# Attention: a new order of row statistics, k's transposes and exponentials, and block ends whose barrier leaves out GpSimd's drain

## The reference, cut to what matters

```python
h = _L0_tok_ref(x)
h = h + _L0_attn_ref(_layernorm(h, axis=-1), wq, wk, wv, wo)
h = h + _L0_ffn_ref(_layernorm(h, axis=-1), w1, w3, w2)
h = h + _L1_attn_ref(_layernorm(h, axis=-1), Wq, Wk, Wv, Wo)
h = h + _L1_ffn_ref(_layernorm(h, axis=-1), gate_up, down)
# one attention, per batch row of 32 tokens:
q, k, v = x @ wq.T, x @ wk.T, x @ wv.T
q, k = rope(q), rope(k)                  # first attention only
att = softmax(causal(q @ k.T * scale))
out = (att @ v) @ wo.T
```

## Time and profile before

| what | us |
|---|---|
| median of 3 runs (lowest, highest) | 2550.73 (2550.29, 2552.34) |
| profiled execution, its time | 2551.09 |
| profiled execution, span of its instructions | 2549.0 |
| TensorE busy (share) | 2265.7 (89%) |
| VectorE busy | 1679.7 (66%) |
| ScalarE busy | 1491.9 (59%) |
| GpSimd busy | 984.8 (39%) |

### The profile page before, as it was taken

One profiled execution on the slowest core, in us unless ns is written; L12 is line 12 of the kernel. 1 busy time (PEld: TensorE's weight loads), 2 busy tenths in 40 slices (PEclk: granted clock), 3 DMA queues, 4 the chain that ended last, 5 costly groups with the idle time before them and its releaser, 6 DMA issues. The chain is left out here.

```text
span 2549.0 us, 43850 instructions
## 1 busy us (share of the span) xinstructions
PE 2265.7 (89%) x13188; PEld 1134.8 (45%) x13188; DVE 1679.7 (66%) x2922; ACT 1491.9 (59%) x2374; POOL 984.8 (39%) x997
## 2 busy tenths in 40 slices
PE   7999999947999994489999995999996899999997
PEld 2333333314666663234444442666662344444443
DVE  6666666635777775575444682566656888788873
ACT  4666666635777775474222662667654666666663
POOL 2222222216766771142000360444433555455552
PEclk9999999978999997699999997999998999999999
DMA  4555454433321110122111223222211111111101
GB/s 120 132 133 131 129 132 131 115 101 125 116 70 62 62 58 29 51 75 76 50 53 49 89 79 101 68 86 74 83 58 43 34 42 46 38 47 44 42 26 50
DMA packets 144174, 194.53 MB, mean 76 GB/s; under 512 B 32549, under 2 KB 76165, under 8 KB 144058
## 3 DMA queue, kind: packets, MB, share of 16 engines
q1 hardware_dynamic: 117434, 159.58, 20.8%
q10 hardware_dynamic: 26624, 33.56, 4.8%
HBM read 125.17 MB, written 42.21 MB: 66 GB/s over the span
## 5 line engine op out<-in xcount | busy, mean ns | idle before, releaser
L330 DVE TENSOR_REDUCE tm_negmax<-tm_s 128x1 f32<-128x512 f32 x512 | 323.2, 678 | 167.5 <-PE tm_s L374 167.3
L291 ACT ACTIVATE tm_prob<-tm_s 128x1024 f32<-128x1024 f32 x256 | 257.8, 1023 | 140.9 <-PE tm_s L394 136.3
L2001 PE MATMUL f_part<-f_xhi,gu 128*128 128x512 f16 x704 | 269.8, 383 | 14.4 <-ACT f_firstg L1822 4.2
L2001 PE MATMUL f_part<-f_xlo,gu 128*128 128x512 f16 x704 | 268.9, 382 | 0.0
L411 PE MATMUL tm_o<-tm_prob,tm_vt 128*64 128x512 f32 x1024 | 255.4, 620 | 0.0
L2023 PE MATMUL f_pz<-dn,f_ghi 128*128 128x512 f16 x704 | 216.3, 383 | 27.7 <-ACT f_zc L1854 27.7
L1791 POOL TENSOR_TENSOR f_firstg<-f_firstg,f_secondg 128x512 f32<-128x512 f32 x88 | 148.6, 1688 | 198.3 <-DVE f_secondg L1897 198.3
L374 PE MATMUL tm_s<-tm_qk 96*128 96x512 f16 x512 | 199.2, 391 | 14.9 <-DMA tm_qk<-tm_xs 14.3
L248 POOL TENSOR_TENSOR tm_hn<-tm_nd,tm_rows 128x1024 f32<-128x1024 f32 x32 | 75.2, 2351 | 311.3 <-DMA tm_rows<-rden 311.3
L394 PE MATMUL tm_s<-tm_qk 98*128 98x512 f16 x512 | 194.1, 382 | 0.6 <-DMA tm_qk<-tm_mrow 0.6
L971 PE MATMUL a_bankB<-a_wqkv,a_xhi 128*128 128x512 f16 x512 | 159.2, 394 | 2.8 <-DVE a_xlo L821 2.8
(11 more groups left out here) (188 smaller groups left out, 5730.9 us busy)
## 6 DMA issues: line engine op xcount, KB each, us to landing
tm_qk<-tm_xs SPq DMA_DIRECT2D x384, 64.0 KB, 2.1
tm_xqk<-in_qk ACTq DMA_DIRECT2D x32, 512.0 KB, 4.5
a_hin<-h SPq DMA_DIRECT2D x64, 256.0 KB, 2.6
a_hres<-h SPq DMA_DIRECT2D x64, 256.0 KB, 2.7
h<-a_hout SPq DMA_DIRECT2D x64, 256.0 KB, 2.0
f_hin<-h SPq DMA_DIRECT2D x64, 256.0 KB, 2.8
f_hres<-h SPq DMA_DIRECT2D x64, 256.0 KB, 2.8
tm_vt<-in_vt ACTq DMA_DIRECT2D x32, 256.0 KB, 2.9
```

The source lines that it names most:

```text
L291: nc.scalar.activation(prob[b][:, 2 * h:2 * h + 2, :], s2[:, i % 2, :, :], ACT.Exp, scale=SCALE).then_inc(exp_done, 1)
L330: nc.vector.tensor_reduce(negmax[u][:, m:m + 1], s1[:, p % BANKS, :], AX.X, ALU.max, negate=True).then_inc(s1_read, 1)
L2001: last = nc.tensor.matmul(part[q % BANKS][:, :], (gate, up)[which][:, j, m * P:(m + 1) * P], xparts[x][u][:, j, :], start=x == 0, stop=x == 1)
```

## The change

Four edits in `attention`, and one on the ends of all blocks:

1. `row_stats`, `mean_variance` and `variance_eps` move on VectorE from the head of the step to behind `shift`, and serve tile n+5 instead of n+4. The wait for the loaded rows moves with them.
2. On TensorE the transposes of k become a function of their own, `transpose_k`, which stands behind `weigh_values(n - 1)` instead of ahead of it.
3. In the attention with rotation `exps(n)` stands on ScalarE ahead of `copy_q(n + 2, u)` instead of behind it. In the other attention ScalarE's order is as before.
4. `nc.Block()` becomes `nc.Block(no_gpsimd_drain=True)` six times: at the end of a block GpSimd issues no drain of its own; on the other four engines what was one drain with the barrier's semaphores is a drain and a semaphore instruction.

The diff, with one of the six block lines; the other five read the same:

```diff
--- before.py
+++ after.py
@@ -133,7 +133,7 @@
 
         MAXIMA_AT = {11: 0, 3: 1}
         VALUES_AT = {7: 0, 11: 1, 15: 2, 3: 3}
-        block = ctx.enter_context(nc.Block())
+        block = ctx.enter_context(nc.Block(no_gpsimd_drain=True))
 
         def unit(i):
 
@@ -737,9 +737,9 @@
                 n = 2 * k + u
                 copy_qT(n + 1)
                 copy_kT(n + 1)
+                exps(n)
                 if rope:
                     copy_q(n + 2, u)
-                exps(n)
                 y_hi(n - 1)
                 if not rope:
                     copy_q(n + 2, u)
@@ -770,8 +770,9 @@
             nc.vector.tensor_tensor(wo[1][:, :, :], wostage[:, :].rearrange("p (r n) -> p r n", r=R),
                                     wo[0][:, :, :], ALU.subtract).then_inc(w_ready, 1)
 
-            def row_stats(t, u):
-                if inside(t, TILES):
+            def row_stats(t, u, half):
+                if inside(t, TILES):
+                    wait(dve, h_in[u], 16 * (half + 1))
                     nc.vector.bn_stats(stats[u][:, :], hin[u][:, :]).then_inc(s["stats_done"], 1)
 
             def mean_variance(t, u):
@@ -874,17 +875,15 @@
 
             def step(k, u):
                 n = 2 * k + u
-                if inside(n + 4, TILES):
-                    wait(dve, h_in[u], 16 * (k + 3))
-                row_stats(n + 4, u)
-                mean_variance(n + 4, u)
-                variance_eps(n + 4, u)
                 k_lo(n + 1, 1 - u)
                 residual(n - 2, u, k - 1)
                 maxes(n)
                 inverse_sums(n - 1)
                 normalise(n - 1)
                 shift(n)
+                row_stats(n + 5, 1 - u, k + 2 + u)
+                mean_variance(n + 5, 1 - u)
+                variance_eps(n + 5, 1 - u)
                 turn(n + 2, u, 0)
                 y_lo(n - 1)
                 turn(n + 2, u, 1)
@@ -899,7 +898,7 @@
             pe.wait_ge(set_up, 8)
             pe.wait_ge(w_ready, KT)
 
-            def transpose_qk(t):
+            def transpose_q(t):
                 if inside(t, TILES):
                     wait(pe, s["qlo_done"], t + 1)
                     wait(pe, s["qT_copied"], t)
@@ -910,6 +909,9 @@
                                                        qs[:, r, f * G:(f + 1) * G, :, :]
                                                        .rearrange("p g a d -> p (g a d)"), ident16[:, :])
                     last.then_inc(s["qT_ready"], 1)
+
+            def transpose_k(t):
+                if inside(t, TILES):
                     wait(pe, s["klo_done"], t + 1)
                     wait(pe, s["kv_copied"], t + 1)
                     for a in range(2):
@@ -1005,8 +1007,9 @@
             def step(k, u):
                 n = 2 * k + u
                 scores(n)
-                transpose_qk(n + 1)
+                transpose_q(n + 1)
                 weigh_values(n - 1, 1 - u)
+                transpose_k(n + 1)
                 project(n + 2, u, bankB[:, 0:DQ], slice(0, DQ), "q_ready", "out_done", n - 1)
                 transpose_y(n - 1)
                 project(n + 2, u, bankC[:, 0:2 * DKV], slice(DQ, DALL), "kv_ready", "kT_act", n + 2)
```

## The result

| | before | changed |
|---|---|---|
| median, 20 runs each | 2551.64 us (2549.36 to 2554.26) | 2555.09 us (2551.96 to 2560.16) |
| ratio | | 1.0014, 95% interval 1.0008 to 1.0020 |
| profiled execution | 2551.09, span 2549.0 | 2553.93, span 2552.1 |

The forecast was 2550.4 with 0.67 on "no change". The time lies inside the range of 2544 to 2556, but the kernel is slower by more than the runs leave in doubt: 3.5 us instead of -0.3.

A forecast was written before the change was run, and what follows sets the result against it. TensorE bounds the second attention's loop; a chain through VectorE and the exponentials would close the first's. Starts +4.8, steps behind them -1.3 and -1.8, loop -2.0, ends 0: -0.3 us, median 2550.4; range 2544 to 2556 (8 in 10).

The forecast's parts named there:

- no change: Whole kernel: time within 0.2% of before, 5.1 us, about what the runs can tell; chance 0.67.
- The loop: First attention's 22 steps: each takes 12.14 us against 12.23, so 2.0 us gained.
- The ring: First attention's loop: `k_lo`, residual, maxima, reciprocal, products, `shift`, `exps`, `copy_q` set the step, 12.14 us.
- The other parts of the table: Parts outside the first loop: first attention's start and first steps +1.4, second's +0.3 us, the rest 0.
- `k_lo` behind `q_lo`: First attention's loop: `k_lo` on VectorE ends 0.28 us after GpSimd's `q_lo`, at 7.13 into the step.
- the rule that it weighed: Rival, first loop: `k_lo` runs whole behind `q_lo`, step 12.28, loop loses 1.1 us, total 2553.5; chance 0.12.
- The starts: Both attentions' starts: moved statistics delay the first `x_lo` by 2.7 and 2.1 us; 4.8 us lost in all.
- The steps behind the starts: First steps of both attentions: waits at k's and the probabilities' transposes go, 1.3 us gained in the first, 1.8 in the second.
- The block ends: Six block ends: GpSimd's drain is hidden behind the last store; 0 taken, between 3 us gained and 0.3 lost.
- the wait for k simply goes: Rival, first loop: step falls to TensorE's 11.56 or near it, 9 to 15 us less, 2537 to 2543; chance 0.13.
- miss its gap: Rival, first loop: `vhi` holds `k_lo`; every step 13.37, total 2577; chance 0.06, wholly or in some steps.
- The ends: Rival, block ends: they do more than forecast, up to 3 us less, 2547; chance 0.04.

## Why the prediction was wrong

**The loop, the step that failed in size and sign.** The ring, the only thing that could decide it, was named link by link, and each link is in the trace. The step "12.14 against 12.23" was mis-sized by 0.21: 1.06 for the way from the exponentials to q's copy is the row of another pair (`exps` to `y_hi`), where the next instruction overlaps the end of `exps` by 0.1; `copy_q` does not (1.17 to 1.18 in the changed kernel and in three experiments with this order). And "nothing in the edits moves `k_hi` against `copy_q`" overlooked that edit 3 brings `turn(..., 1)` into `cross`, 0.10. Against a margin of 0.09 a step, 0.21 turns the sign: 22 x 0.21 = 4.6 us, more than the 3.7 between forecast and result. The other parts of the table miss theirs by -1.2, +0.7, +5.1, -5.1, -1.4 and +1.0, which nearly cancel; that the total is off by under 0.2% is in part luck.

**`k_lo` behind `q_lo`**: right, 0.28 forecast and 0.29 measured. The forecast took the 0.28 as speaking against the rule that it weighed (the Trainium skill, SBUF — State Buffer, "SBUF: two separate sides": whichever starts first keeps the shared ports and the other fully blocks). It does not refute it: started 0.13 before `q_lo` ends, `k_lo` takes no longer than alone and ends at the same place as when it starts half a microsecond earlier. So it looks as if it waited wholly, with only its first 0.13 us beside the other; that `q_lo` gives way 0.13 before its recorded end would give the same rows. The row at hand, not the rule plus a full duration, gave the number.

**The starts**: `x_lo` was forecast 2.7 and 2.1 later and came, against each stage's start, 3.3 and 1.3 later. That both go to the end in full was wrong. In the first attention 3.0 us of it reach tile 0's scores and 0.4 tile 1's: the first step, which was 16.27 us long with 3.4 us of half clock in it, takes 13.70 at full clock. That is chance as much as mechanism, since the same first attention in another profile had half clock there and came 2.5 later.

**The steps behind the starts**: the two waits for k's transposes in the second attention, 1.8 us, went as forecast. The rest of the -4.8 is the clock's, as in the kernel before with half a microsecond of delay (-3.0). By this account nothing is left there of the 1.3 us by which `x_lo` comes later.

**The block ends**: 0.75 us lost and not 0.

**What had no term**: half clock in a stage behind the change. With +5.1 there, -3.0 and +0.5 further on, as in the delayed kernel before, it is some 2.6 of the profile's 3.4 us; the edits' own work gives the other 0.8, since -1.8 in the second attention's first steps and -1.4 in the rest of it (1.2 of them its loop, where a step takes 9.855 and not the 9.91 that the forecast kept) stand against the loop's +2.6. The full clock in the first attention's first step is in these 0.8 too, so the clock's part is rather larger.

**The rivals**: "the wait for k simply goes" is the right picture of edits 1 and 2 (2537 to 2543 forecast for it, 2536.7 measured) and fell by edit 3 alone. `k_lo` did not miss its gap. The ends did the opposite of more.

**Open**: why the first step of the first attention is shorter with edit 3 even where it has as much half clock; why either of edits 1 and 2 shortens the second attention's step; whether the clock's part is the same in all timed runs as in the profiled ones (the changed kernel was profiled twice, with the same length of the stage; the spread of 8 us within its runs says that not all are alike); why q's copy never overlaps the exponentials.

## What to carry to other kernels

Where a change opens one ring and closes another, work out both to a tenth of a microsecond, take the price of each link from a row of that very pair of instructions, and ask what every instruction behind the moved one now falls on. An edit should be priced by itself: here two of three were worth 11 and 15 us each, and the third cost all of it. And a difference of 0.1 to 0.2% may come from a stage that nobody touched: compare stage by stage, clock beside time, before explaining it by the edit.

## What was not expected of the hardware

- Half a microsecond of delay in one place made the stage behind it 5.1 us longer in one kernel, and 2.8 us made it 5.1 shorter in another: the stage is 513.6 to 513.8, 515.6, 516.1 to 516.2 or 518.8 to 519.0 us long in 18 profiles, for the same instructions, by when it starts against the changes of the granted clock.
- Three more waits that had been met over a microsecond before, in front of an instruction, made it start 0.19 and 0.08 us behind the one it depends on, by turns, instead of 0.03: 0.11 us a step.
- The block end without GpSimd's drain is longer at each of six ends, 1.65 us instead of 1.54 at the one shown.
